# Another order of ScalarE's and TensorE's lists, and loads counted in four groups, in a graph-attention, Mamba and expert kernel

## The reference

```
x = x + attention(layernorm(x), adj)          # softmax over neighbours, two matmuls with 256x256
x = x + mamba2(layernorm(x))                  # projections, 4-tap conv, silu, decays exp(cumsum), y @ W_out @ W_lin
h_r = mask_r @ layernorm(x), r = 1..4         # masks from adj; sum over r of h_r @ weight[r] + bias
x = x + that
x = x + experts(layernorm(x))                 # gate, argmax, one of 8 experts 256 -> 1024 -> 256, with a capacity
```

## Time and profile before

| | us |
|---|---|
| median of three timed runs | 3772.7 (3771.9 to 3774.0) |
| the profiled execution's own time | 3761.8 |
| its span, first to last instruction | 3760.1 |
| mean granted TensorE clock | 0.982 of full speed |
| TensorE busy | 3484.0 (93%) |
| VectorE busy | 2585.9 (69%) |
| ScalarE busy | 1763.4 (47%) |
| GpSimd busy | 1814.9 (48%) |

### The profile page before, as it was taken

The page is one execution under the profiler, slowest core; times in us unless marked ns, Lnnn a source line. Parts: engine busy times, 40 slices in busy tenths (PEclk is TensorE's granted clock), DMA queues, the critical chain, the costliest instruction groups (busy, mean ns, idle before and its releaser), DMA issues.

```text
span 3760.1 us, 64606 instructions
## 1 busy us (share of the span) xinstructions
PE 3484.0 (93%) x20028; PEld 2881.9 (77%) x20028; DVE 2585.9 (69%) x7429; ACT 1763.4 (47%) x3625; POOL 1814.9 (48%) x2010
## 2 busy tenths in 40 slices
PE   5999999999999999999999999999699999999998
PEld 4777777777777777777777777777588888888887
DVE  4888787888778878887878878788534444444444
ACT  2555555555555555555555555555223233232322
POOL 2445545454454545454454545445345454554543
PEclk8999999999999999999999999999899999999999
DMA  3111121111111111111111111111055555555554
GB/s 99 36 35 45 36 36 39 38 40 34 48 34 36 39 36 40 36 48 34 36 39 37 41 35 45 36 36 37 16 191 192 190 194 195 196 194 190 194 194 133
DMA packets 166001, 301.92 MB, mean 80 GB/s; under 512 B 37376, under 2 KB 138240, under 8 KB 147776
## 3 DMA queue, kind: packets, MB, share of 16 engines
q0 software_dynamic: 38272, 196.40, 15.3%
q1 hardware_dynamic: 92864, 71.37, 6.2%
q10 hardware_dynamic: 34816, 33.56, 5.9%
HBM read 248.61 MB, written 52.65 MB: 80 GB/s over the span
## 4 chain that ended last, share of the span: by engine, by line
PE 56%; DVE 22%; issue 9%; POOL 7%; ACT 4%; ACTq 1%; SPq 0%; DMA 0%; DVEq 0%; POOLq 0%
PE bank L1289 13%; PE bank L1303 13%; PE bank L1080 12%; DVE conv L788 6%; PE bank L1063 4%; PE bank L1241 3%; DVE y L936 3%; PE bank L1156 3%; POOL masks L449 3%; DVE y L941 2%; POOL row L435 2%; DVE stats L769 2%; POOL rstd L435 2%; PE bank L1181 2%; DVE xn L779 1%
## 5 line engine op out<-in xcount | busy, mean ns | idle before, releaser
L708 ACT ACTIVATE decay<-bank,w_up 128x256 f32<-128x256 f32 x568 | 268.9, 473 | 699.7 <-PE bank L1289 699.7
L1063 PE MATMUL bank<-xn1T,w_in 128*128 128x256 f32 x2304 | 523.3, 381 | 2.5 <-ACT xn1T L570 0.7
L1289 PE MATMUL bank<-zs,w_up 128*128 128x256 f32 x2272 | 503.5, 380 | 0.6 <-ACT zs L570 0.6
L1303 PE MATMUL bank<-w_dn,decay 128*128 128x256 f32 x2272 | 502.1, 379 | 0.0
L788 DVE SCALAR_TENSOR_TENSOR conv<-bank,conv_w,conv 128x255 f32<-128x255 f32 (+2 forms) x960 | 461.6, 481 | 34.8
L1063 PEld LDWEIGHTS bank<-xn1T,w_in 128*128 128x128 f32 x2304 | 432.6, 190 | 60.6 <-ACT xn1T L570 0.9
L1289 PEld LDWEIGHTS bank<-zs,w_up 128*128 128x128 f32 x2272 | 432.6, 190 | 60.0 <-issue 0.9
L1080 PE MATMUL bank<-w_rel,hT 128*128 128x256 f32 x2048 | 471.7, 384 | 0.7 <-ACT hT L570 0.7
L1303 PEld LDWEIGHTS bank<-w_dn,decay 128*128 128x128 f32 x2272 | 426.2, 190 | 55.1
L1012 DVE TENSOR_TENSOR hT<-bank,w_dn 128x256 f32<-128x256 f32 x142 | 60.3, 425 | 535.3 <-PE bank L1303 535.3
L1080 PEld LDWEIGHTS bank<-w_rel,hT 128*128 128x128 f32 x2048 | 380.8, 191 | 57.9 <-issue 9.9
(11 more groups left out here) (220 smaller groups left out, 6330.6 us busy)
## 6 DMA issues: line engine op xcount, KB each, us to landing
token_rows<-row SPq DMA_DIRECT2D x64, 258.0 KB, 2.8
xT_sb<-in_xT ACTq DMA_DIRECT2D x64, 256.0 KB
adj_sb<-in_adj SPq DMA_DIRECT2D x64, 256.0 KB, 3.0
x_sb<-in_x ACTq DMA_DIRECT2D x64, 256.0 KB, 2.7
adjt_sb<-in_adjT SPq DMA_DIRECT2D x64, 256.0 KB, 3.0
out<-row SPq DMA_DIRECT2D x64, 256.0 KB, 2.2
w_in<-token_rows,idc POOLq DMA_INDIRECT x142, 4.8
out<-hT,ids POOLq DMA_INDIRECT x142, 2.4
```

Of the source, the lines that this page charges most:

```text
L708: nc.scalar.activation(hid(f), bank[f % 4][:, 0:GROUP], ACT.Relu, bias=b1[q % 2][:, f:f + 1]).then_inc(hid_ready, 1)
L1063: ins = mm(dst, w_in[:, k, first:first + P], xn1T[:, k, :], start=k == 0, stop=k == DK - 1)
L1289: ins = mm(bank[f % 4][:, 0:GROUP], w1[i][:, k, f * P:(f + 1) * P], xgT[:, k, :], start=k == 0, stop=k == DK - 1)
L1303: ins = mm(bank[4 + j][:, 0:D], hid(f)[:, j * P:(j + 1) * P], w2[i][:, f, :], start=f == 0, stop=f == FB - 1)
```

## The change

Three things are changed.

1. ScalarE's list. The copies to `hT` are taken one by one: the first right behind Ln, then `s12`, then the second and third, the first `zs`, the fourth, then B and C, `xs`, the second `zs`, `z` and `wh`. Silu's table is asked for behind Ln and Exp's behind `wh`; `g` comes behind Exp's, then `prob` and `probT`, then all eight decays.
2. TensorE's list. `relate` and `attend` are cut in halves. The scores go to bank 7, between the halves of relate(0); the first half of relate(1) and the transposes of `prob` are in front of the first `expo`; `attend(1)` is behind the transposes of `xn3`; `out_made` is in front of the running counts.
3. The start. Four semaphores count the loads. `gat_in`: the attention's weight and vector, first on SP. `mix_in` (nine loads) and `rel_in` (five) follow on SP behind the first adjacency load; `out_in` (W_out, norm, W_lin) goes on ScalarE's queue. The scaling and the transposes of W_out are done in step 0, its products with W_lin in step 1, behind the projections. The first load of x is no longer behind a wait for all loads.

```
+                if is_first(b1_):
+                    load_all(sp, mix_loads, mix_in)
+                    load_all(sp, rel_loads, rel_in)
...
                     nc.scalar.activation(dt_ln[:], dt_exp[:], ACT.Ln, bias=1.0).then_inc(dt_act, 1)
+                    nc.scalar.preload_act_table(ACT.Silu)
+                if b3_ is not None:
+                    h_part(0, b3_)
...
+                if b3_ is not None:
+                    h_part(1, b3_)
+                    h_part(2, b3_)
                 if b2_ is not None:
                     act.wait_ge(proj_made, 5 * b2_ + 4)
                     need(act, yz_ready, 2 * b2_)
                     nc.scalar.activation(zs[:, 0:2, :], bank[5][:, :], ACT.Silu).then_inc(zs_ready, 1)
...
+                if b3_ is not None:
+                    h_part(3, b3_)
...
+                    need(act, hp_made, b1_)
+                    for t in range(T):
+                        ins = nc.scalar.activation(wh[:, t, :], bank[t][:, 0:D], ACT.Copy, scale=rstd[0][:, t:t + 1])
+                    ins.then_inc(wh_ready, 1)
+                nc.scalar.preload_act_table(ACT.Exp)
                 if b2_ is not None:
                     act.wait_ge(g_made, b2_ + 1)
                     need(act, m_ready, 4 * b2_)
                     copy(g[:], bank[5][:, 0:TRI + T * H]).then_inc(g_ready, 1)
...
+                if is_first(b1_):
+                    dve.wait_ge(out_in, 16 * len(out_loads))
+                    for c in range(XB):
+                        ins = v.tensor_scalar(w_out[:, c, :], w_out[:, c, :], norm_w[:, c:c + 1], None, ALU.mult)
+                    ins.then_inc(w_out_scaled, 1)
...
-            pe.wait_ge(loads, 16 * len(small))
+            pe.wait_ge(gat_in, 16 * len(gat_loads))
...
+                if is_first(b2_):
+                    pe.wait_ge(conv_ready, 3)
+                    pe.wait_ge(dt_act, 1)
+                    pe.wait_ge(w_outT_ready, 1)
+                    for c in range(XB):
+                        for k in range(DK):
+                            ins = mm(bank[6 + c // 2][:, (c % 2) * D:(c % 2 + 1) * D],
+                                     w_outT[:, k, c * P:(c + 1) * P], w_lin[:, k, :], start=k == 0, stop=k == DK - 1)
+                    ins.then_inc(w_proj_made, 1)
...
+                if b3_ is not None:
+                    pe.wait_ge(hT_ready, 4 * b3_ + 3)
+                    relate(0, range(0, 2))
+                    pe.wait_ge(hT_ready, 4 * b3_ + 4)
...
+                if b3_ is not None:
+                    relate(0, range(2, R))
...
                 if b3_ is not None:
-                    pe.wait_ge(hT_ready, 4 * b3_ + 4)
-                    relate(0)
-                if b2_ is not None:
-                    expo(range(0, 4), b2_, b1_)
-                if b3_ is not None:
-                    relate(1).then_inc(gy_made, 1)
+                    relate(1, range(0, 2))
...
+                if b2_ is not None:
+                    expo(range(0, 4), b2_)
+                if b3_ is not None:
+                    relate(1, range(2, R)).then_inc(gy_made, 1)
+                if b2_ is not None:
+                    expo(range(4, H), b2_)
```

More of the change, by code:

```diff
@@ L305, in graph_mamba_moe, with load_all, is_first @@
         ]
[L306 to L309, removed]
+        rel_loads += [(gate_b[:, t, :], gb) for t in range(T)]
+        def load_all(eng, pairs, done):
+            for dst, src in pairs:
+                eng.dma_start(dst[:] if not isinstance(dst, bass.AP) else dst, src).then_inc(done, 16)
+        def is_first(b):
+            return isinstance(b, int) and b == 0
         x_v = x_d.rearrange("b (t p) d -> b p t d", p=P)
@@ L372, in _ @@
         def _(sp):
-            for dst, src in small:
-                sp.dma_start(dst[:] if not isinstance(dst, bass.AP) else dst, src).then_inc(loads, 16)
+            load_all(sp, gat_loads, gat_in)
             def step(b1_, b2_, b3_, turn_):
@@ L463, in step @@
                 if b2_ is not None:
-                    if isinstance(b2_, int) and b2_ == 0:
-                        pool.wait_ge(loads, 16 * len(small))
+                    if is_first(b2_):
+                        pool.wait_ge(ids_set, 16)
+                        pool.wait_ge(mix_in, 16 * len(mix_loads))
                         pool.dma_start(w_up[0][:], io["moe_up"][0:P, :]).then_inc(up_in[0], 16)
@@ L664, in step @@
                     ins.then_inc(prob_ready, 1)
-                for h in range(H):
-                    if b2_ is not None:
+                    act.wait_ge(prob_turned, b1_ + 1)
+                    need(act, hp_made, b1_)
+                    copy(probT[:], bank[0][:, :]).then_inc(probT_ready, 1)
+                if b2_ is not None:
+                    for h in range(H):
                         act.wait_ge(expo_made, 8 * b2_ + h + 1)
@@ L670, in step @@
                         nc.scalar.activation(decay[:, h, :], bank[EXPO[h % 4]][:, 0:TRI], ACT.Exp).then_inc(decay_ready, 1)
-                    if h == 3 and b1_ is not None:
-                        act.wait_ge(prob_turned, b1_ + 1)
-                        need(act, hp_made, b1_)
-                        copy(probT[:], bank[0][:, :]).then_inc(probT_ready, 1)
                 if b3_ is not None:
@@ L743, in _ @@
             ins.then_inc(built_v, 1)
-            for c in range(XB):
-                ins = v.tensor_scalar(w_out[:, c, :], w_out[:, c, :], norm_w[:, c:c + 1], None, ALU.mult)
-            ins.then_inc(prep_v, 1)
             dve.wait_ge(built_v, 1)
@@ L1242, in step @@
                                      start=j == 0, stop=j == XB - 1)
+                if b2_ is not None:
+                    pe.wait_ge(y2s_ready, b2_ + 1)
+                    if b1_ is not None:
+                        pe.wait_ge(xn1T_ready, b1_ + 1)
+                    for t in range(T):
+                        ins = mm(bank[5][:, t:t + 1], y2s[:, t * P:(t + 1) * P], ones_row[:, 0:1], start=True,
+                                 stop=True)
+                    ins.then_inc(out_made, 1)
                 if turn_ is not None and turn_[1] == turn_[2] - 1:
@@ L1255, in step @@
                     ins.then_inc(cum_made, 1)
-                if b2_ is not None:
-                    pe.wait_ge(y2s_ready, b2_ + 1)
-                    if b1_ is not None:
-                        pe.wait_ge(xn1T_ready, b1_ + 1)
-                    for t in range(T):
-                        ins = mm(bank[5][:, t:t + 1], y2s[:, t * P:(t + 1) * P], ones_row[:, 0:1], start=True,
-                                 stop=True)
-                    ins.then_inc(out_made, 1)
             rounds(pe, step)
```

172 lines of the change are left out of this document (93 added, 79 removed).

## The result

| | median, us | runs | profiled execution | span | mean clock |
|---|---|---|---|---|---|
| before, beside it | 3772.3 | 3762.2 to 3774.0 | 3761.8 | 3760.1 | 0.982 |
| after | 3670.5 | 3668.3 to 3672.0 | 3668.3 | 3666.5 | 0.990 |

The ratio is 0.9738 (95% interval 0.9715 to 0.9760): 102 us faster, where 60 had been predicted.

A forecast was written before the change was run, and what follows sets the result against it. TensorE, busy but for a 2.10 us hole, was taken as the bound, with VectorE's chain second. Start 21, pairs 14 and clock 25 summed to 60 us off the 3772.7 median: 3713 us, range 3680 to 3744.

The forecast's parts named there:

- The hole: TensorE's 2.10 us wait for hT in the masked sums of full steps: gone, 0 to 0.2 us left.
- The clock, 25 us: Full steps: falls of the granted clock to 1.2 GHz vanish as TensorE's longest idle shortens; 25 us, bounds 0 and 25.
- Rival 1: Full steps: the falls of the clock stay, giving 3738 us; chance 0.20.
- The start, 21 us: Before step 1: TensorE awaits two loads instead of all, step 1 begins earlier; net 21 us, bounds 5 and 25.
- The pair, 14 us: Two neighbouring steps: row's wait removed against later decays, about 0.45 us a pair, 31 pairs; bounds nothing and 42 us.
- rival 2: VectorE's chain in the steps moves by the whole row waits: 42 us instead of 14, 3685 us; chance 0.12.
- g behind the Exp load, at nothing: ScalarE's list: xdt waits 0.4 us for g, hidden in VectorE's 2.48 us wait for decays; no cost.
- cum and out_made: Routing step: swapping them takes route's wait off neither, costing about 0.1 us, counted in the 0.45.
- The base: Timed median 3772.7 lies 11 us above the profiled execution; the same 60 us was taken off it.
- Slower, decays too late: ScalarE's list before the first decay: table loads holding longer delay weigh 1.3 us a step, 3794 us; chance 0.07.

The follow-up runs named there:

- e9: Kernel before, with TensorE making the last group of the first half of the masked sums (four products) twice: 3737.8 us against 3755.9, ratio 0.9949.
- e3: Changed kernel, but relate(1) undivided behind expo(0:4) as before, prob's transposes still ahead of it: 3795.3 us, ratio to before 1.0078.
- e5: Changed kernel with ScalarE's old list up to z (both zs, bT, cT, s12 in front of the hT copies): 3915.9 us, ratio to before 1.0410.
- e6: Kernel before with only ScalarE's early hT copies, Silu's table loaded between copies and zs: 3940.5 us, ratio 1.0469.
- e15: Kernel before with only ScalarE's early hT copies, Silu's table loaded ahead of the first copy: 3787.1 us, ratio 1.0072.
- e1: Kernel before with only the changed start (counted loads, first attention early, w_proj's products in step 1): 3745.4 us against 3763.5, ratio 0.9948.
- e13: Changed kernel with one additional one-column GpSimd product (about 0.15 us) ahead of the masks: 3660.5 us.
- e14: Changed kernel with three additional one-column GpSimd products (about 0.45 us) ahead of the masks: 3678.3 us.
- e7: Changed kernel, but ScalarE copies g ahead of wh and of Exp's table load, as before: 3732.3 us.
- e11: Changed kernel, but the routing counts stand in front of the products that sum y2s, as before: 3667.6 us.
- e10: Changed kernel, but GpSimd's two x2b additions stand in front of its wait for xdt, so its masks start earlier: 3668.5 us.
- e4: Changed kernel, but prob's transposes stand behind relate(1)'s second half and probT is copied behind the fourth decay: 3649.0 us.
- e8: Changed kernel with a new order around the decays, VectorE making xdt ahead of z, e and nmax: 3593.9 us, ratio to before 0.9551.

## Why the prediction was wrong

*The hole*: right. Gone, as computed.

*The clock, 25 us*: right. 23.6 in the traces, and e9 has it alone at 18 (timed) to 24 (traces). Rival 1, the falls stay, is refuted for this list; e3, e5, e6 and e15 show that it was close, since they all have the falls again, e15 with no single wait above 1.25 us. That waits up to 1.2 us would be harmless, as the prediction took it, has held here; no run shows why, and the term owes something to luck.

*The start, 21 us*: right in sum, 19.4. The first product came at 7.0 (6.9 predicted) and attend at 11.5 (11.2). Step 1 began at 32.6, 2.2 us ahead of the prediction, in spite of a table load in front of s12 that I had not seen (ScalarE idle to 15.82, then 1.28 us). Step 1 then lost 4.4 us (39.6 against 35.2) where 2.3 were predicted. VectorE's wait for w_proj's products and its copy took 2.2, as computed. But e1, which has them too, lost only 1.8, so the rest came with the new lists: TensorE waits 2.54 us for prob in front of the first expo, and from 51 to 63 us it works at 1.2 GHz, a granted clock of 0.50, where e1 has 0.86 in the same part of the step. How much each of the two took was not separated.

*The pair, 14 us*: **the step that failed**, by its size. The mechanism is the predicted one, row's wait against later decays, but the pair gained 1.51 us, not 0.45. So the term was 46.8 us instead of 14, above even its upper bound of 42. Offsets against before within a pair, counted from the first dt_abs (the earlier trace rows and the rows above), with the prediction's:

| | predicted | measured | difference of the increments |
|---|---|---|---|
| weigh, routing step | +0.20 | +0.07 | -0.13 |
| row, routing step | -0.47 | -0.68 | -0.08 |
| weigh, other step | +0.31 | -0.22 | -0.32 |
| row, other step | -0.36 | -1.39 | -0.50 |
| end of the pair | -0.45 | -1.51 | -0.03 |

Of the 1.06 us, 0.41 in the fourth line is weigh's short form. In the other step the decays come 0.62 us later behind xdt, and so behind the masks: weigh's first product, which started 0.07 us ahead of a mask before, now starts 0.56 behind one, and the second starts 0.04 ahead of the next and keeps its 0.95 us. e13 and e14 show that such a shift is worth such time. Nothing in the prediction foresaw it, so this part is luck. The rest of that line is that I used weigh's busy 2.24 us where row can start 2.17 us behind weigh's start. The third line holds some 0.16 us that the second weigh had itself waited for its decays, and prob, which ended 1.30 us behind the start of nmax, not 1.43 as before. The first is TensorE, which reached expo 0.07 us later instead of 0.2. Four small numbers, all of one sign, were taken as one "about"; in effect rival 2 came true, with its chance of 0.12 too low. Row moved by 0.68 and by another 0.71 us in the two steps, the whole of its wait in each, though in the other step only with weigh's short form. e3 shows that row's wait depends on this one cut of relate(1).

*g behind the Exp load, at nothing*: right for the move itself, but I had looked at the wrong side of it. e7 shows that leaving g in its old place would have cost 62 us, more than the pair term gives: a new wait of ScalarE for TensorE's later g, with prob behind it. The 14 us stood on that move without my naming it.

*cum and out_made*: nothing, as e11 confirms.

*The base*: 11 us were carried from the median over the profiled execution. The changed kernel's median is only 2.2 above its profile, and its runs lie close together where those of before scatter by 12 us. That scatter goes with the clock: over 42 runs of before beside the experiments the mean granted clock falls from 0.986 in the fastest (3751.0 us) to 0.978 in the slowest (3773.3 us). So the base was most likely falls of the clock too, and should have gone with them. So the 42.6 us between 3713 and 3670.5 are 31.4 of the steps (32.8 of the pair less 1.4 of the clock), 8.7 of the base, 3.8 behind the steps, less 1.6 of the start, and 0.3 of rounding.

*Slower, decays too late*: refuted for the change, since each table load is followed at once by work. In e5 and e6 the decays do come late, but through waits for hT, z and zs, not through table loads.

## What to carry to other kernels

When a hole in an engine's list is closed, ask where its idle time goes: here the same 2 us brought clock drops in some steps wherever they stood together, and none once cut into waits of about 1 us with several us of work between them. Lists that feed each other have to be moved together; with one side or a piece of it in its old order the kernel was 27 to 179 us slower than before either was touched. An instruction that moves in a list takes the wait in front of it along, so price that wait and all that is queued behind it, not only the instruction. Where a term is a small difference of larger ones, take start-to-start distances, not busy times, and widen it to the whole wait that is being removed.

## What the runs showed of the hardware

*Weigh's products and GpSimd's masks hold each other up, but unequally.* For a product that starts behind a mask, the distance from the mask's start plus what the product takes over its 0.96 us is nearly constant: 0.06 + 0.40, 0.11 + 0.35, 0.23 + 0.24, in e13 (1290.03 against 1289.62, 1.02 us) 0.41 + 0.06, and in e10 0.13 + 0.40: 0.46 to 0.53 us. A product 0.52 us behind (e13, 1249.18 against 1248.66) keeps its 0.96 us. The other way round a mask that starts 0.04 to 0.14 us behind a product takes 2.16 to 2.27 instead of 1.49 us: 0.67 to 0.78 more, where the product ends 0.80 to 0.91 us behind the mask's start. The Trainium skill (SBUF — State Buffer, SBUF: two separate sides) has the rule that whichever of the two starts first holds the shared ports for its whole instruction. For a product that starts first the trace nearly agrees; for a mask that starts first it does not: the product that began at 1255.07 ended at 1256.43, before the mask did (1256.50), and was held only 0.4 us.

*The clock.* Longer waits of TensorE go with more falls, but no length of a single wait separates the two. The granted clock in 200 to 2400 is 1.00 with regular waits of about 1 us and less (changed kernel, e4, e7, e8) and of 1.2 to 1.4 us (e9). It is 0.99 with 2.1 and 2.3 us (before), 0.97 with 1.4 and 2.4 us (e3) or 2.1 and 2.3 us (e5), and 0.93 with 2.6 us (e6). Yet e15 has 0.97, with a wait of 1.25 us that is no longer than e9's. And before has the hole in each of its 62 steps and a fall in 14; in e15 the clock falls in some of the steps with the lone 1.25 us wait and in some with both waits, 1.25 and 0.91 us, and not in others of either kind. What decides in which step the clock falls stays open. The Trainium skill (TensorE: Matmul & The Clock Gate, A second HAM failure mode: psum-queue depth-cycling) reports short idles between groups of matmuls as a cause of swings. e15 agrees with that; the changed kernel, whose waits of 0.98, 0.38 and 0.52 us lie within nine, has none in its regular steps.
